# Weighting the expert outputs in the tile loop and adding them into the normalised rows in memory, in a state-space and mixture-of-experts kernel

## The chip, the cores and the metric

The kernel is one launch on one core of a Trainium2 chip. The number is the device time of one execution, in microseconds (us). The kernel before was run three times: 622.35, 623.21 and 623.45 us, median 623.21.

## The reference

Two blocks follow each other, on 8 sequences of 512 tokens with 256 features (4,096 tokens in all). The second is the one that the change touches.

```python
x = x + layernorm(s4d_block(layernorm(x)))                 # the first block gives x1
x = x + layernorm(moe_block(layernorm(x)))

def moe_block(x, ln_g, ln_b, rW, rb, W1, b1, W2, b2):      # 8 experts, 2 chosen per token
    z = layernorm(x) * ln_g + ln_b
    probs = softmax(z @ rW + rb)
    topv, topi = top_k(probs, 2)
    w = one_hot_weights(topv, topi) / max(sum, 1e-08)
    hid = gelu(z @ W1[e] + b1[e])                           # erf form
    outs = hid @ W2[e] + b2[e]
    return x + sum_e(outs[e] * w[e])
```

For each token the kernel needs n = layernorm(x1), the outputs y of its two experts, their weights w, and at the end x1 + layernorm(n + w0 y0 + w1 y1).

## The kernel before, in words

A block of 512 tokens (one sequence b) lies in SBUF as 128 partitions x 4 rows x 256 floats, 512 KB. Five instruction streams are written by hand: SP (`block.sync`, issues the plain DMAs), ACT (`scalar`), DVE (`vector`), POOL (`gpsimd`), PE (`tensor`). Each runs in its written order; semaphores order them against each other. There is no scheduler.

**The first block and the routing** (L306 to L995). For each b the first block ends in `xs[b]` (x1) and ACT writes `zn` (L516), the normalised rows n, in four buffers: b = 0, 2, 4 share one, b = 1, 3, 5 the next, b = 6 and 7 have their own (`buf`, L285). DVE picks two experts per row and works out where each row belongs in the expert's region, and POOL scatters the 4 rows of 128 tokens twice, once per choice, into `z_rows` in DRAM (L1116, 64 indirect DMAs). A row of `z_rows` has two more floats, the token's number and its second expert. SP stores x1 to `x1_dram` (`store_x1`, L344) and loads the experts' weights (`load_expert`, L269) as buffers come free.

**The tile loop** (`tiles`, L256; 71 tiles of 128 rows of one expert, six to a round of the hardware loop). For tile t SP loads 128 rows (`load_z`, L377). DVE finds out whether the row came from the first or the second choice (`flag`, L1005) and writes the row number where its result goes, token + 4096 x choice, to `dest` (L1008). PE transposes (L1316), ACT applies gain and bias (L584), DVE splits into a high and a low part (L1013, L1015), PE makes the first product (L1329), DVE adds the bias (L1023), ACT takes the gelu (L598), PE transposes (L1338), ACT and DVE split (L592, L1028), PE makes the second product (L1348). DVE copies `dest` to `dst` (L1037) and writes the product plus bias to `y_sb` (L1038). POOL sends the 128 rows of `y_sb` to `y_rows` in DRAM with an indirect DMA (`scatter_y`, L1146), 1 KB per row. There are two buffers of each tile, and the stages of several tiles overlap: in round i PE transposes the input of tile i + 2 and makes the second product of tile i - 1. `scatter_y(t)` waits for `y_ready` and for the landing of the scatter of t - 1:

```python
pool.wait_ge(sem("y_ready"), t + 1)
if not early(t):
    pool.wait_ge(sem(f"y_out{1 - q}"), (t + q) * 8)
```

**The tail.** When all scatters have landed, SP loads both results of each token (`ya`, L410, 16 loads of 512 KB, throttled two pairs at a time) and x1 of b = 0 to 3 (L408, 2 MB). POOL makes diagonal matrices of the weights (`weights`, L1161, products with the identity), PE sums the two results times their weights (`mix`, L1356, 128 matmuls), ACT makes n again from x1 (`base`, L603), DVE adds the two (L1048) and takes mean and variance (L1052, L1057), ACT takes the root (L614), DVE makes scale and shift (`scale`, L1060), ACT applies them (L618), DVE adds x1 (`add`, L1071), SP stores (L414).

## Time and profile before

| | |
|---|---|
| median of 3 runs | 623.21 us |
| the profiled execution | 619.89 us |
| its span, first to last instruction | 618.3 us |
| PE busy | 481.2 us (78%) |
| DVE busy | 462.4 us (75%) |
| ACT busy | 347.4 us (56%) |
| POOL busy | 227.2 us (37%) |
| mean granted TensorE clock | 0.903 |

The profile is one execution. Its span leaves 1.6 us of its own time outside, and its own time is 3.3 us below the median. Busy time counts what an engine executes, not its waits. "Idle before" in a row is the time that the engine stood still ahead of that instruction, with what ended it. An average over the span says little here, because the three stages (first block and routing, tile loop, tail) have different limits; each is read in its own window.

### The profile page before, as it was taken

The numbers are of one execution on the slowest core, as the hardware profiler recorded it, in microseconds if no ns is written. First come the engines' busy times: TensorE is split into PE (matmuls) and PEld (weight loads), VectorE is DVE, ScalarE is ACT, GpSimd is POOL, SyncE is SP. The second block draws the span as 40 slices with busy tenths as digits, with TensorE's granted clock in tenths as the row PEclk, the third lists the DMA queues.
The fourth block names the chain that finished last, engine by engine and source line by source line (L and its number), as shares of the span: only waits on it lengthen the run. The fifth ranks groups of instructions, "written<-read, shape, count | busy, mean of one in ns | idle before, by whom it ended". The sixth has DMA issues, their size and how long they took to land. (4 is left out here: it accounts for less than half of the span.)

```text
span 618.3 us, 12465 instructions
## 1 busy us (share of the span) xinstructions
PE 481.2 (78%) x2841; PEld 416.0 (67%) x2842; DVE 462.4 (75%) x1412; ACT 347.4 (56%) x751; POOL 227.2 (37%) x195
## 2 busy tenths in 40 slices
PE   0379899769979673132899999999999999956850
PEld 0139888659868573131788898889888888845640
DVE  6999877997986953863577777778778777832885
ACT  6983755654765566522455555555555555561584
POOL 0000676236775854653023232232232232342410
PEclk9998999989989885555799999999999999996995
DMA  6206600201110878336222222222222222119923
GB/s 186 88 0 255 222 1 1 68 2 69 44 61 36 287 261 296 95 126 223 85 69 77 77 72 81 68 72 81 68 69 84 68 74 79 60 43 368 344 103 136
DMA packets 36827, 69.56 MB, mean 113 GB/s; under 512 B 7520, under 2 KB 23648, under 8 KB 36160
## 3 DMA queue, kind: packets, MB, share of 16 engines
q1 hardware_dynamic: 30320, 51.48, 25.1%
q0 software_dynamic: 6480, 17.77, 8.1%
q8 instruction: 11, 0.18, 0.1%
q14 instruction: 16, 0.13, 0.1%
HBM read 42.02 MB, written 27.21 MB: 112 GB/s over the span
## 5 line engine op out<-in xcount | busy, mean ns | idle before, releaser
L1152 POOL DMA_INDIRECT y_rows<-y_sb,dst x71 | 76.5, 1077 | 194.0 <-DVE y_sb L1038 140.1
L1329 PE MATMUL psum<-ws,z_hl 128*128 x426 | 119.9, 417 | 0.8 <-DVE z_hl L1015 0.8
L1348 PE MATMUL psum<-ws,h_hl 128*128 x852 | 115.9, 285 | 0.1
L1348 PEld LDWEIGHTS psum<-ws,h_hl 128*128 128x128 f32 x852 | 103.5, 189 | 0.3 <-issue 0.3
L1116 POOL DMA_INDIRECT z_rows<-zn,pos x64 | 75.5, 1180 | 41.3 <-DVE pos L878 24.8
L1329 PEld LDWEIGHTS psum<-ws,z_hl 128*128 128x128 f32 x426 | 76.9, 193 | 16.0 <-issue 1.5
L592 ACT CAST h_hl<-psum 128x512 fp32r<-128x512 f32 x71 | 41.7, 587 | 76.0 <-PE psum L1338 76.0
L1023 DVE TENSOR_TENSOR hb<-psum,b1r 128x512 f32<-128x512 f32 x71 | 49.1, 692 | 37.3 <-issue 34.0
L584 ACT ACTIVATE z_f<-psum,gb 128x128 f32<-128x128 f32 x142 | 57.1, 452 | 15.7 <-PE psum L1316 13.8
L598 ACT ACTIVATE hg<-hb 128x512 f32<-128x512 f32 x71 | 44.9, 632 | 33.3 <-DVE hb L1023 33.3
L1219 PE MATMUL psum<-pm,ft 128*128 128x256 f32 x256 | 60.2, 395 | 0.4 <-DVE tmp L837 0.3
L1248 PE MATMUL psum<-yf,it 128*128 128x256 f32 x256 | 59.3, 387 | 0.0
L1219 PEld LDWEIGHTS psum<-pm,ft 128*128 128x128 f32 x256 | 50.2, 198 | 8.3 <-issue 1.2
L1248 PEld LDWEIGHTS psum<-yf,it 128*128 128x128 f32 x256 | 48.6, 194 | 6.5 <-POOL yf L1103 0.2
L1028 DVE TENSOR_TENSOR h_hl<-psum,h_hl 128x512 fp32r<-128x512 f32 x71 | 48.3, 680 | 1.3 <-ACT h_hl L592 1.3
L1364 PE MATMUL psum<-ya,diag 128*128 (+1 forms) x128 | 31.9, 410 | 18.1 <-DMA ya<-y_rows 13.7
L1316 PE MATMUL psum<-ident,z_in 128*128 128x128 f32 x142 | 28.8, 286 | 21.5 <-DMA z_in<-z_rows 20.0
L1338 PE MATMUL psum<-ident,hg 128*128 128x128 f32 x284 | 43.0, 274 | 0.0
L1338 PEld LDWEIGHTS psum<-ident,hg 128*128 128x128 f32 x284 | 35.7, 141 | 9.9 <-issue 0.2
L1364 PEld LDWEIGHTS psum<-ya,diag 128*128 128x128 f32 x128 | 26.0, 207 | 23.7 <-issue 19.9
L1101 POOL TENSOR_TENSOR yf<-yf,tmp 128x512 f32<-128x512 f32 x16 | 20.4, 1274 | 40.8 <-DVE rs L930 24.3
L1109 POOL TENSOR_TENSOR pm<-xn 128x512 f32<-128x512 f32 x8 | 10.3, 1285 | 66.2 <-ACT xn L441 66.2
(205 smaller groups left out, 847.1 us busy)
## 6 DMA issues: line engine op xcount, KB each, us to landing
z_in<-z_rows SPq DMA_DIRECT2D x71, 129.0 KB, 2.0
w_raw<-in_dram SPq DMA_DIRECT2D x16, 512.0 KB, 5.4
ya<-y_rows SPq DMA_DIRECT2D x16, 512.0 KB, 5.5
xs<-in_dram SPq DMA_DIRECT2D x8, 512.0 KB, 5.4
x_dram<-xs SPq DMA_DIRECT2D x8, 512.0 KB, 7.0
x1m<-x_dram SPq DMA_DIRECT2D x2, 2048.0 KB, 8.4
out_dram<-acc SPq DMA_DIRECT2D x8, 512.0 KB, 2.6
b1r<-in_dram SPq DMA_DIRECT2D x8, 256.0 KB, 4.5
```

Source lines behind the costliest of these rows:

```text
L584: last = nc.scalar.activation(z_f[:, k], ps_z[q][:, k], ACT.Identity, bias=gb[:, 1, k:k + 1], scale=gb[:, 0, k:k + 1])
L598: nc.scalar.activation(hg[q][:, :], hb[:, :], ACT.Gelu).then_inc(sem("hg_ready"), 1)
L1023: V.tensor_tensor(hb[:, :], ps_h[q], b1r[:, bass.ds(e, 1)].rearrange("p a f -> p (a f)"), ALU.add).then_inc(sem("hb_ready"), 1)
L1028: V.tensor_tensor(h_hl[q][:, 1], ps_t[q], h_hl[q][:, 0].bitcast(F32), ALU.subtract).then_inc(sem("h_split"), 1)
L1116: pool.indirect_dma_start(z_rows, bass.IndirectOffsetOnAxis(ap=pos[row.par][:, i // 4, i % 4:i % 4 + 1], axis=0), zn[buf(row.b)][:, i % 4] ...
L1152: pool.indirect_dma_start(y_rows, bass.IndirectOffsetOnAxis(ap=dst[q][:, 0:1], axis=0), y_sb[q][:, :], None).then_inc(sem(f"y_out{q}"), 16)
L1219: last = TE.matmul(fw[u][c][:, k], ft[:, c, t, kt * P:(kt + 1) * P], pm[row.b][:, c, t], start=t == 0, stop=t == 1)
L1248: last = TE.matmul(iv[c][:, j * H:(j + 1) * H], it[:, c, k, j * P:(j + 1) * P], yf[row.par][:, c, k], start=k == 0, stop=k == KT - 1)
L1329: last = TE.matmul(ps_h[q], z_hl[q][:, a, k], w_at(e1, c, k * F, F), start=n == 0, stop=n == 5)
L1338: last = TE.transpose(ps_t[q][:, k], hg[q][:, k * P:(k + 1) * P], ident[:, :])
L1348: last = TE.matmul(ps_y[q], h_hl[q][:, a, k], w_at(e2, c, 1024 + k * H, H), start=n == 0, stop=n == 11)
L1364: last = TE.matmul(ps_mix[par][:, k * H:(k + 1) * H], diag[par][:, c, k], ya[:, bass.ds(n, 1), c, k].rearrange("p a h -> p (a h)"), start= ...
```

## The change

`y_rows` now holds one row per token (4,096, and 128 that catch padding) instead of two. SP stores the normalised rows `zn` of each b there, right behind x1, and each of the buffers may be written again only when its store has landed (ACT). The weights are written to `w_rows` in DRAM, one float per token and choice. In the tile loop POOL gathers the 128 weights of a tile (`gather_w`), ACT multiplies the tile's result by them into a third pair of buffers `yw`, POOL copies the token numbers to `dst` (DVE did a copy of this kind before), and the scatter to `y_rows` adds to what stands there (`compute_op=ALU.add`). In the tail SP loads one row per token, and the diagonal matrices, the products on PE, ACT's `base` and DVE's addition of the two are gone; the last addition of x1 moves from DVE to POOL. Expert 4 is loaded behind expert 5.

```diff
-TRASH = 2 * B * T
+TRASH = B * T
...
+            def store_rows(lo, hi):
+
+                for b in range(lo, hi):
+                    sp.wait_ge(sem("x1_ready"), b + 1)
+                    sp.dma_start(x1_dram[:, b], xs[b][:, :, :]).then_inc(sem("x1_stored"), 16)
+                    sp.wait_ge(sem("zn_ready"), b + 1)
+                    sp.dma_start(y_tok[:, b], zn[buf(b)][:, :, 0:H]).then_inc(sem(f"zn_stored{buf(b)}"), 16)
+                sp.wait_ge(sem("x1_stored"), 16 * hi)
+
+
+            store_rows(0, 4)
+            load_expert(sp, 5)
...
             sp.wait_ge(sem("kf_mm"), 2)
             sp.wait_ge(sem("fwd_mm"), 16)
             load_expert(sp, 4)
-
-            def store_x1(lo, hi):
-                for b in range(lo, hi):
-                    sp.wait_ge(sem("x1_ready"), b + 1)
-                    sp.dma_start(x1_dram[:, b], xs[b][:, :, :]).then_inc(sem("x1_stored"), 16)
-                sp.wait_ge(sem("x1_stored"), 16 * hi)
-
-
-            store_x1(0, 4)
-            sp.wait_ge(sem("zn_ready"), 4)
-            load_expert(sp, 5)
-            store_x1(4, 6)
+            store_rows(5, 6)
             sp.wait_ge(sem("zn_ready"), 6)
             sp.wait_ge(sem("mult_done"), 2 * B)
             load_expert(sp, 6)
...
-            store_x1(6, 8)
-            sp.wait_ge(sem("zn_ready"), B)
-            sp.wait_ge(sem("x1_ready"), B)
+            store_rows(6, 8)
...
+            sp.dma_start(y_rows[TRASH:TRASH + P, :], zpad[:, 0:H]).then_inc(sem("trash_set"), 16)
...
+            sp.wait_ge(sem("wgt_ready"), 1)
+            sp.dma_start(w_rows.rearrange("(c p n) o -> p c (n o)", c=2, p=P),
+                         wgt[:, 0:2].rearrange("p c b k -> p c (b k)")).then_inc(sem("w_stored"), 16)
...
             for n in range(B):
-                if n >= 2:
-                    sp.wait_ge(sem(f"y0_in{n % 2}"), 16 * (n // 2))
-                    sp.wait_ge(sem(f"y1_in{n % 2}"), 16 * (n // 2))
-                if n == 3:
+                if n == 2:
+                    sp.wait_ge(sem("x1_in"), 16)
                     sp.dma_start(x1m[:, 0:4], x1_dram[:, 0:4]).then_inc(sem("x1_in"), 16)
-                for c in (1, 0):
-                    sp.dma_start(ya[:, n, c], y_tok[:, B - 1 - n, c].rearrange("p (k h) -> p k h", k=4)).then_inc(
-                        sem(f"y{c}_in{n % 2}"), 16)
+                sp.dma_start(yr[:, n], y_tok[:, B - 1 - n]).then_inc(sem(f"y_in{n}"), 16)
...
                     act.wait_ge(sem(f"scattered{row.par}"), 64 * (row.b - row.par))
+                    act.wait_ge(sem(f"zn_stored{row.par}"), 8 * (row.b - row.par))
...
+                t, q = i - 2, par
+                if live(t):
+                    act.wait_ge(sem("y_ready"), t + 1)
+                    gate(act)
+                    act.wait_ge(sem(f"w_in{q}"), (t - q) * 8 + 16)
+                    if not early(t):
+
+                        act.wait_ge(sem("dst_set"), t)
+                    nc.scalar.activation(yw[q][:, :], y_sb[q][:, :], ACT.Identity, scale=wt[q][:, 0:1]).then_inc(sem("yw_ready"), 1)
...
-
-
...
+            def close(n):
+                act.wait_ge(sem("m_var"), n + 1)
+                nc.scalar.activation(rm[:, n % 2, 0, :], mvm[n % 2][:, :, 1], ACT.Sqrt, bias=eps[:, 0:1]).then_inc(sem("m_sd"), 1)
+                act.wait_ge(sem("m_rs"), n + 1)
                 for k in range(4):
...
+                    last = nc.scalar.activation(acc[:, n, k], yr[:, n, k], ACT.Identity,
+                                                bias=rm[:, n % 2, 2, k:k + 1], scale=rm[:, n % 2, 1, k:k + 1])
                 last.then_inc(sem("m_fin"), 1)
...
+            for n in range(B):
+                close(n)
...
+                    V.tensor_copy(row_of[:, bass.ds(t, 1)], z_in[q][:, H:H + 1])
...
                     if not early(t, 2):
-                        dve.wait_ge(sem(f"y_out{q}"), (t - q) * 8)
-                    gate(dve)
-                    V.tensor_copy(dst[q][:, :], dest[:, bass.ds(t, 1)])
+                        dve.wait_ge(sem("yw_ready"), t - 1)
                     V.tensor_tensor(y_sb[q][:, :], ps_y[q], b2r[:, bass.ds(e, 1)].rearrange("p a f -> p (a f)"),
                                     ALU.add).then_inc(sem("y_ready"), 1)
 
...
+            def spread_of(n):
+                dve.wait_ge(sem(f"y_in{n}"), 16)
+                if n > 1:
+                    dve.wait_ge(sem("m_sd"), n - 1)
                 for k in range(4):
-                    last = V.bn_stats(st[:, par, k, :], acc[:, bass.ds(b, 1), k].rearrange("p a h -> p (a h)"))
-                last.then_inc(sem("m_stat"), 1)
-                dve.wait_ge(sem("m_stat"), b + 1)
-                gate(dve)
+                    last = V.bn_stats(st[:, n % 4, k, :], yr[:, n, k])
+                do(last)
                 for k in range(4):
-                    last = V.bn_aggr(mvm[par][:, k, :], st[:, par, k, :])
+                    last = V.bn_aggr(mvm[n % 2][:, k, :], st[:, n % 4, k, :])
                 last.then_inc(sem("m_var"), 1)
 
...
+            def scale(n):
+                par = n % 2
+                dve.wait_ge(sem("m_sd"), n + 1)
+                if n > 1:
+                    dve.wait_ge(sem("m_fin"), n - 1)
+                do(V.reciprocal(rm[:, par, 1, :], rm[:, par, 0, :]))
+                do(V.scalar_tensor_tensor(rm[:, par, 2, :], mvm[par][:, :, 0], -1.0, rm[:, par, 1, :], ALU.mult, ALU.mult))
+                V.tensor_tensor(rm[:, par, 2, :], rm[:, par, 2, :], xb[:, B - 1 - n], ALU.add).then_inc(sem("m_rs"), 1)
+
+            spread_of(0)
+            for n in range(B):
+                if n + 1 < B:
+                    spread_of(n + 1)
+                scale(n)
...
+            def gather_w(t, q):
+
+                pool.wait_ge(sem("dest_ready"), t + 1)
+                if not early(t, 2):
+                    pool.wait_ge(sem(f"w_in{q}"), (t - q) * 8)
+                gate(pool)
+                G.tensor_copy(widx[q][:, :], dest[:, bass.ds(t, 1)]).then_inc(sem("widx_set"), 1)
+                pool.wait_ge(sem("widx_set"), t + 1)
+                gate(pool)
+                pool.indirect_dma_start(wt[q][:, 0:1], None, w_rows,
+                                        bass.IndirectOffsetOnAxis(ap=widx[q][:, 0:1], axis=0)).then_inc(sem(f"w_in{q}"), 16)
+
             def scatter_y(t, q):
-                pool.wait_ge(sem("y_ready"), t + 1)
+
+                pool.wait_ge(sem("yw_ready"), t + 1)
                 if not early(t):
-
                     pool.wait_ge(sem(f"y_out{1 - q}"), (t + q) * 8)
                 gate(pool)
+                G.tensor_copy(dst[q][:, :], row_of[:, bass.ds(t, 1)]).then_inc(sem("dst_set"), 1)
+                pool.wait_ge(sem("dst_set"), t + 1)
+                gate(pool)
                 pool.indirect_dma_start(y_rows, bass.IndirectOffsetOnAxis(ap=dst[q][:, 0:1], axis=0),
-                                        y_sb[q][:, :], None).then_inc(sem(f"y_out{q}"), 16)
-
+                                        yw[q][:, :], None, compute_op=ALU.add).then_inc(sem(f"y_out{q}"), 16)
+
+            pool.wait_ge(sem("w_stored"), 16)
+            gather_w(0, 0)
+            gather_w(1, 1)
+            for b in range(B - 2):
+                pool.wait_ge(sem(f"zn_stored{b % 2}"), 16 * (b // 2 + 1))
+            for i in (2, 3):
+                pool.wait_ge(sem(f"zn_stored{i}"), 16)
+            pool.wait_ge(sem("trash_set"), 16)
             scatter_y(0, 0)
-            with pool.Fori(0, (TILES - 1) // 2) as j:
+            gather_w(2, 0)
+            with pool.Fori(0, (TILES - 3) // 2) as j:
                 scatter_y(j * 2 + 1, 1)
+                gather_w(j * 2 + 3, 1)
                 scatter_y(j * 2 + 2, 0)
...
+                gather_w(j * 2 + 4, 0)
+            scatter_y(TILES - 2, 1)
+            scatter_y(TILES - 1, 0)
+
+            def add(n):
+                pool.wait_ge(sem("m_fin"), n + 1)
+                if n % 4 == 0:
+                    pool.wait_ge(sem("x1_in"), 16 + 4 * n)
+                G.tensor_tensor(acc[:, n], acc[:, n], x1m[:, B - 1 - n], ALU.add).then_inc(sem("m_out"), 1)
+
+            for n in range(B):
+                add(n)
...
-            pe.wait_ge(sem("y_ready"), TILES)
-            mix(0, 0)
-            mix(1, 1)
-            with pe.Fori(1, B // 2) as j:
-                mix(j * 2, 0)
-                mix(j * 2 + 1, 1)
```

In the loop on POOL there was this, for two tiles (`dst` holds row numbers, `y_sb` the result):

```order
L1156 ISA
L1150 REGISTER_ALU [waits y_ready]
L1152 DMA y_rows<-y_sb_163,dst_145 8320x256 [waits y_out0]
L1147 REGISTER_ALU
L1152 DMA y_rows<-y_sb_162,dst_144 8320x256 [waits y_ready,y_out1]
L1156 REGISTER_ALU
L1156 COMPARE_AND_BRANCH
```

The same place in the changed kernel, for one of the two tiles (`yw` is the weighted result, `wt` the weights, `widx` their row numbers):

```order
L1122 ISA [waits yw_ready,y_out1]
L1122 COPY dst_144<-row_of 128x1
L1125 DMA y_rows<-yw_151,dst_144 4224x256 [waits dst_set]
L1106 REGISTER_ALU
L1108 REGISTER_ALU [waits dest_ready]
L1110 ISA [waits w_in0]
L1110 COPY widx_147<-dest 128x1
L1113 DMA wt_149<-w_rows,widx_147 128x1 [waits widx_set]
L1138 REGISTER_ALU
L1138 COMPARE_AND_BRANCH
```

Where POOL had one DMA per tile behind one set of waits, it has two copies and two DMAs, each DMA behind a wait for the copy ahead of it, and the first copy behind the landing of the scatter before.

In ACT's tile loop one tile of the changed kernel reads as follows:

```order
L586 ACTIVATE z_f<-psum,gb 128x128 [waits z_split,tz_mm]
L586 ACTIVATE z_f<-psum,gb 128x128
L594 CAST h_hl_177<-psum 128x512 [waits l2_mm,th_mm]
L600 ACTIVATE hg_174<-hb 128x512 [waits th_mm,hb_ready]
L609 ACTIVATE yw_152<-y_sb_170,wt_150 128x256 [waits y_ready,dst_set,w_in1]
```

The last row is new. It is the weighting of the tile whose number is three below that of the gelu ahead of it, and it waits for POOL's copy for the tile before it (`dst_set`), which in turn stands behind a landing.

On DVE the tail of one sequence had a 1,024-element addition ahead of the statistics and one behind; now it is this:

```order
L1031 BN_STATS st<-yr 128x6 [waits m_sd,y_in4]
L1031 BN_STATS st<-yr 128x6 x3
L1034 BN_AGGR mvm_183<-st 128x2 [waits dve_seq]
L1034 BN_AGGR mvm_183<-st 128x2 x3
L1042 RECIPROCAL rm<-rm 128x4 [waits m_fin,m_sd]
L1043 SCALAR_TENSOR_TENSOR rm<-mvm_184,rm 128x4 [waits dve_seq]
L1044 TENSOR_TENSOR rm<-rm,xb 128x4 [waits dve_seq]
```

The statistics of a sequence (here the fifth) stand ahead of the scale and shift of the one before it.

## Rows read from the trace of the kernel before

**Rows 1.** The page, part 2: busy tenths in 40 slices of 15.5 us.
```profile
PE   0379899769979673132899999999999999956850
...
PEclk9998999989989885555799999999999999996995
```
**Rows 2.** Stretches: PE, PEld, DVE, ACT, POOL busy, PEclk, DMA share, GB/s.
```profile
289.00:306.00 17.00, 13.94 (x59) 10.75 (x59) 8.63 (x27) 6.78 (x15) 0.05 (x1) 0.65 0.45 162
306.00:550.00 244.00, 241.60 (x1648) 215.50 (x1646) 189.05 (x542) 134.26 (x271) 74.52 (x69) 1.00 0.24 73
556.20:618.30 62.10, 31.87 (x128) 26.04 (x128) 38.24 (x104) 29.85 (x63) 13.58 (x8) 0.77 0.62 237
```
**Rows 3.** Timeline of the loop: start, duration, engine, line, idle before.
```profile
440.25 0.43 DVE L1038 TENSOR_TENSOR y_sb<-psum,b2r 128x256 f32<-128x256 f32 x1
...
441.49 1.12 POOL L1152 DMA_INDIRECT y_rows<-y_sb,dst  x1 [3.22 <-DVE y_sb L1038]
...
443.11 1.64 PE L1329 MATMUL psum<-ws,z_hl 128*128 x6
...
444.85 1.12 POOL L1152 DMA_INDIRECT y_rows<-y_sb,dst  x1 [2.23 <-DMA y_rows<-y_sb,dst]
...
446.55 1.65 PE L1329 MATMUL psum<-ws,z_hl 128*128 x6
```
**Rows 4.** `y_rows` in the trace: what POOL waited for (us, times), time to landing.
```profile
  DMA y_rows<-y_sb,dst: 48.3, 21
...
DMA to landing us min/median/max: 2.4/2.6/10.8
```
**Rows 5.** Timeline of POOL: a memset, one routing scatter, the first and last scatters.
```profile
0.22 0.10 POOL L1437 MEMSET const-float32-0.0<- 128x1 f32 x1 [0.22 <-issue]
...
149.51 0.96 POOL L1116 DMA_INDIRECT z_rows<-zn,pos  x1 [0.30 <-issue]
...
305.95 1.18 POOL L1152 DMA_INDIRECT y_rows<-y_sb,dst  x1 [21.81 <-DVE y_sb L1038]
...
553.67 0.96 POOL L1152 DMA_INDIRECT y_rows<-y_sb,dst  x1 [2.22 <-issue]
```
**Rows 6.** The page, part 6: DMA issues, KB each, us to landing.
```profile
z_in<-z_rows SPq DMA_DIRECT2D x71, 129.0 KB, 2.0
```
**Rows 7.** Groups in the window 306:550: busy, mean ns, idle before.
```profile
L598 ACT ACTIVATE hg<-hb 128x512 f32<-128x512 f32 x68 | 43.0, 632 | 29.6 <-DVE hb L1023 29.6
...
L1038 DVE TENSOR_TENSOR y_sb<-psum,b2r 128x256 f32<-128x256 f32 x70 | 29.7, 424 | 0.0
```
**Rows 8.** Timeline at the loop's start: ACT's gelu of the fourth tile.
```profile
307.42 0.63 ACT L598 ACTIVATE hg<-hb 128x512 f32<-128x512 f32 x1 [0.59 <-DVE hb L1023]
```
**Rows 9.** Timeline of the tail: one sequence's statistics, the last sequence's end.
```profile
569.30 1.41 DVE L1052 BATCH_NORM_STATS2 st<-acc 128x6 f32<-128x256 f32 x4
570.85 0.38 DVE L1057 BATCH_NORM_AGGREGATE mvm<-st 128x2 f32<-128x6 f32 x4
...
610.67 0.28 ACT L614 ACTIVATE rm<-mvm,eps 128x4 f32<-128x4 f32 x1
...
611.71 2.07 ACT L618 ACTIVATE acc<-acc,rm 128x256 f32<-128x256 f32 x4 [0.76 <-DVE rm L1068]
613.81 1.23 DVE L1074 TENSOR_TENSOR acc<-acc,x1m 128x1024 f32<-128x1024 f32 x1 [1.01 <-ACT acc L618]
```
**Rows 10.** The page: GB/s of the slices; POOL's additions and products (mean ns).
```profile
GB/s 186 88 0 255 222 1 1 68 2 69 44 61 36 287 261 296 95 126 223 85 69 77 77 72 81 68 72 81 68 69 84 68 74 79 60 43 368 344 103 136
...
L1101 POOL TENSOR_TENSOR yf<-yf,tmp 128x512 f32<-128x512 f32 x16 | 20.4, 1274 | 40.8 <-DVE rs L930 24.3
...
L1166 POOL TENSOR_TENSOR diag<-ident,wgt 128x1024 f32<-128x1024 f32 x8 | 15.1, 1897 | 20.4 <-PE psum L1364 20.4
```
**Rows 11.** SP's waits in total: what stood between its issues.
```profile
SPq L341 <- PE psum L1219: 83.3, 1, 83.3
...
SPq L388 <- DMA z_rows<-zn,pos: 4.6, 1, 4.6
```

127 lines of the change are left out of this document (16 added, 111 removed).

## The prediction, written before the changed kernel ran

> **What bounds the kernel now.** I read the slices of the page first, then the stretches, then the timeline inside one stretch.
>
> From 309 us on PE is busy nearly all the time and has its full clock (tenths of 9 and 1.00, 2.4 GHz) up to the tail [rows 1, 2]. In the loop proper (306 to 550 us) it is busy 241.6 of 244.0 us. PE's first product of one tile starts at 443.11 and that of the next at 446.55: 3.44 us. Over the whole loop the scatters start 70 times between 305.95 and 553.67 [rows 5], which is 3.54 us per tile. So PE is the bound of the loop. What matters more for this change is the runner-up. A scatter on POOL may start only when the one before has landed. Between 441.49 and 444.85 it was that landing that released POOL [rows 3], and it was so 21 times [rows 4]. Such an interval is 3.36 us: the scatter lands 2.6 us after its start [rows 4], and some 0.8 us pass until the next starts. The same 0.8 us stands between the end of `y_sb` (440.25 + 0.43 = 440.68) and the scatter at 441.49 [rows 3], so it is what POOL needs from a released wait to the start of an indirect DMA. The chain of scatters thus has 3.54 - 3.36 = 0.18 us of slack per tile. POOL looks idle two thirds of the loop, but its idle time is the flight of the scatters.
>
> The tail, from the last landing (553.67 + 2.4 = 556.1) to 618.3, takes 62.2 us [rows 2, 5]. There a chain passes PE, DVE and ACT for each sequence, behind 8 MB of loads.
>
> **What the change takes away: the tail.** Per sequence the diagonal matrices, 16 matmuls, ACT's base and two DVE additions go. The new tail, step by step. SP issues the rows of sequences 0 and 1 in its order, then 2 MB of x1, then those of 2. These are 3.67 MB at 344 to 368 GB/s [rows 10], 10.2 us, and some 2 us until a landing is seen (as z_in [rows 6]): 12.3. DVE's statistics of sequence 2 (1.41 + 0.38 with a wait between them, 1.9 [rows 9]) stand ahead of the scale of sequence 1: 14.2. Scale and shift take 0.75 (from 610.67 + 0.28 to 611.71), ACT applies in 2.1: sequence 1 is through at 17.3. From there on each sequence costs ACT root, wait for DVE, apply: 610.67 to 613.78, 3.1, say 3.15 [rows 9]; six of them end at 36.2. DVE's statistics (1.9) lie beside ACT's apply (2.1), so they cost nothing; were ACT faster, DVE would be next. The last addition is now on POOL. Its 512-element addition takes 1.27, its 1,024-element product with broadcast operands 1.90 [rows 10]: I take 2 x 1.27 = 2.5, low end 1.9, and POOL hides all but the last. The store after it and the end take 618.3 - 615.04 = 3.2 [rows 9]. Sum 36.2 + 0.1 + 2.5 + 3.2 = 42.0 us instead of 62.2: **20.2 us gained** (39 to 46 us are possible).
>
> **What it adds: the loop.** Per tile:
> - DVE copies the token number and no longer the row number: nil. Its result now waits for `yw` of two tiles earlier, which matters only if ACT is late.
> - ACT weights the result, 128 x 256. The same shape takes DVE 0.42 [rows 7], ACT's half of z_f 0.45; with it ACT has some 2.5 of 3.5 us busy. Its idle time before the gelu (29.6 us in 68 tiles [rows 7]) covers it. It is queued ahead of the next tile's z_f, so a late `dst_set` holds up everything.
> - POOL: the chain scatter to scatter gets a copy and its semaphore. A small operation on POOL takes 0.10 [rows 5]; with its start and its semaphore I take 0.3 (low 0.15; high 0.9, if a wait before the DMA costs another 0.8).
> - The add: the DMA engines must also read the row that they add to. No row shows such a DMA. Low end 0, since the trace has the plain write and nothing makes a read and write shorter than it; high end 2.0, a whole load of the same 128 rows, as z_in [rows 6]. I take 0.6, nearer to the plain scatter, since the 128 rows are independent and their reads overlap.
>
> Chain per tile: 3.36 + 0.3 + 0.6 = **4.26, taken as 4.25 us**, 0.7 above what PE needs. The second bound is POOL's own queue: scatter 1.1, copy 0.15, 0.8 until the gather starts, gather 1.1, copy 0.15, 0.8 until the next scatter: 4.1. With the shortest DMAs (0.96 [rows 5]) and 0.75 for a start it is 3.8. The gather lies in the scatter's flight as long as the flight is longer; so the two bounds are not summed.
>
> The Trainium skill (Collectives: The Full Stack, "The bandwidth ceiling: the fold count and why AG ≠ RS ≠ AR") says that the add in a DMA engine costs nothing itself and only doubles the reads; with the 436 GB/s of its DMA page (DMA: Bandwidth & Descriptors, "Anatomy of one DMA") that is 0.3 us for 128 KB, an estimate from the page, and by it the chain would be 3.96 and POOL's queue of 4.1 the bound: 643 instead of 655. No row here shows an adding DMA.
>
> Start: the gelu of the fourth tile ends at 308.05 [rows 8], ACT's first weighting at 308.5, and with copy and start the first scatter goes at 309.5 instead of 305.95. Then 70 x 4.25 = 297.5: the last starts at 607.0 and lands at 610.2, 54.1 later than before.
>
> **Before the loop.** Eight stores of 512 KB are added. SP waited 83.3 us in one piece for the last forward product [rows 11], and the first of them and of x1 now go into that gap. ACT's new wait for a stored buffer should be covered, since the same buffer is scattered first, which takes eight DMAs of 1.26. Expert 4 is behind expert 5, and expert 7's load behind 512 KB more (1.4 us). SP waited 4.6 us for the scatters ahead of the first z_in [rows 11], which covers the padding store. I put the whole at 1 us (0 to 5).
>
> **Sum.** 618.3 + 54.1 - 20.2 + 1 = 653.2, and with the 1.6 us outside the span 654.8: **655 us**, against 619.9 of the profiled execution. The runs' median was 3.3 us above that; the forecast stands for both within that.
>
> **Rivals.**
> 1. *The add is cheap and POOL's queue is the bound*, 4.1 us per tile: 309.5 + 287 + 2.9 = 599.4; with 42.0, 1 and 1.6 it is 644. For it: the DMA engines are used to a quarter in the loop [rows 2].
> 2. *The add is dear.* It costs a whole load more, 2.0: 5.66 per tile, last landing 710.3, in all 755. A longer descriptor program on POOL for it (1.6 instead of 1.1) would give 4.6 to 4.8 and 680 to 695. For it: each row must be read before it is written, and POOL must describe both.
> 3. *The loop stays PE's (faster than before).* If the add costs under 0.2 us and the gather's and copies' starts are hidden by POOL's sequencer, the interval is 3.65: last landing 309.5 + 255.5 + 2.6 = 567.6, in all 612. It decides at an interval of 3.8 us, where 309.5 + 266 + 2.8 + 44.6 = 623. For it: a DMA behind another starts 0.30 us after it [rows 5] instead of 0.8. Against it: both new DMAs wait for a copy that ends just before.
> 4. *PE's clock falls* in the new gaps: the first product took 1.65 at full clock [rows 3]; at 1.2 GHz a tile needs about twice its 3.44 at most, nearer 6.1, and all takes about 785. Against it: at tenths of 6 and 7 of busy time the clock stayed at 9 [rows 1].
> 5. *The change doesn't shorten the tail*: its loads (x1 ahead of rows 2 to 7) starve DVE, and it stays at 62: 675.
>
> **How the numbers follow.** Forecast (4.2 to 4.5 per tile) 0.38; rival 1 0.20; rival 2 0.22; rival 3 0.14; rival 4 0.02; rival 5 0.04. The likeliest case alone gives 636 to 690. The range leaves out most of rival 3 and the upper part of rival 2: 620 to 735. About 0.2% (1.2 us) is what a measurement of this kernel can tell from no change. Rival 3 is faster nearly wholly (0.13); between 622 and 624.5 lies almost nothing (0.03); slower 0.84.
>
> **What would show it.** Right: scatters over 4 us apart, POOL waiting for the landing of `y_rows`; PE's idle time in the loop ended by ACT or DVE, PE at 80 to 85% there and its clock full; ACT's `yw` released by POOL's `dst`; tail of about 42 us with POOL's addition at its end. If POOL is busy or starting something all the time and the landing is never last, rival 1 is right; if scatters land 4 us or more after their start, rival 2. Wrong: scatters 3.5 us apart, PE at 99%.

## The result, and the profile after

The changed kernel takes 729.70 us (median of 4 runs, 727.96 to 731.32), the kernel before, run beside it, 622.78 (620.24 to 623.45): a ratio of 1.171, interval 1.168 to 1.174. The sign was forecast and the range (620 to 735) holds it, but the forecast of 655 is 75 us too low. The profiled execution has a span of 729.3 us, 111.0 more than before.

The page of the changed kernel, busy tenths in slices of 18.2 us (compare [rows 1]):
```profile
PE   0678998798986330698877878778787877761000
...
POOL 0004572457576475145556566565656656664253
PEclk9989999898997555699999999999999999995555
```
In the loop PE is at 7 to 8 tenths and its clock stays at 9. The loop's stretch says it in numbers (PE, PEld, DVE, ACT, POOL busy, PEclk, DMA share, GB/s; compare [rows 2]):
```profile
306.00:640.00 334.00, 269.20 (x1613) 210.19 (x1611) 179.76 (x533) 153.70 (x332) 194.64 (x255) 0.99 0.32 51
```
PE fell from 99% to 81% of the loop at full clock, POOL rose from 31% to 58%. The costliest groups of the page (busy, mean ns, idle before and its releaser; compare [rows 7]):
```profile
L1125 POOL DMA_INDIRECT y_rows<-yw,dst x71 | 113.7, 1601 | 59.1 <-DVE dest L992 46.8
...
L1113 POOL DMA_INDIRECT wt<-w_rows,widx x71 | 71.3, 1004 | 59.2 <-POOL widx L1110 52.4
...
L609 ACT ACTIVATE yw<-y_sb,wt 128x256 f32<-128x256 f32 x71 | 36.1, 509 | 96.0 <-DMA wt<-w_rows,widx 96.0
...
L1110 POOL COPY widx<-dest 128x1 uint32 (+1 forms) x71 | 57.8, 814 | 13.3 <-DMA w_rows<-wgt 13.3
```
The adding scatter occupies POOL 1.60 us; it was 1.0 to 1.2 before. A copy of one number per partition takes 0.81. One tile on POOL, with the next scatter (start, duration, idle before; compare [rows 3]):
```profile
439.13 1.60 POOL L1125 DMA_INDIRECT y_rows<-yw,dst  x1 [0.82 <-DVE dest L992]
440.17 0.77 POOL L1110 COPY widx<-dest 128x1 uint32 x1
441.72 1.00 POOL L1113 DMA_INDIRECT wt<-w_rows,widx  x1 [0.79 <-POOL widx L1110]
443.30 0.18 POOL L1122 COPY dst<-row_of 128x1 uint32 x1 [0.58 <-DMA y_rows<-yw,dst]
444.31 1.59 POOL L1125 DMA_INDIRECT y_rows<-yw,dst  x1 [0.83 <-POOL dst L1122]
```
From 439.13 to 444.31 it is 5.18 us. The row of POOL's own work, scatter to copy 1.04, copy 0.77, start 0.79, gather 1.00, copy 0.18, start 0.83, is 4.6 of that. The 0.58 left is the wait for the landing of the scatter before. The copy `widx` lies partly inside the scatter's 1.60 and is slow there; the copy `dst`, alone, takes 0.18. Between 330 and 640 us POOL stood still before this copy in 56 tiles, 23.8 us in all, 0.4 each. The profile names the landing as what ended it in 10 of them and names nothing in 46, so this trace alone doesn't settle what binds; the run without gathers below does.

The beginning of the loop on POOL (compare [rows 5]):
```profile
302.82 0.18 POOL L1110 COPY widx<-dest 128x1 uint32<-128x1 uint32 x1 [13.25 <-DMA w_rows<-wgt]
...
315.93 1.77 POOL L1125 DMA_INDIRECT y_rows<-yw,dst  x1 [0.82 <-POOL dst L1122]
```
One sequence of the tail, DVE, ACT and POOL, up to the next addition (compare [rows 9]):
```profile
694.02 0.28 ACT L617 ACTIVATE rm<-mvm,eps 128x4 f32<-128x4 f32 x1
694.19 2.34 POOL L1150 TENSOR_TENSOR acc<-acc,x1m 128x1024 f32<-128x1024 f32 x1 [3.40 <-ACT acc L620]
694.33 0.18 DVE L1042 RECIPROCAL rm<-rm 128x4 f32<-128x4 f32 x1 [0.59 <-ACT rm L617]
694.54 2.00 DVE L1043 SCALAR_TENSOR_TENSOR rm<-mvm,rm 128x4 f32<-128x4 f32 x1
696.58 0.16 DVE L1044 TENSOR_TENSOR rm<-rm,xb 128x4 f32<-128x4 f32 x1
...
696.78 2.07 ACT L620 ACTIVATE acc<-yr,rm 128x256 f32<-128x256 f32 x4 [2.48 <-DVE rm L1044]
698.93 2.34 POOL L1150 TENSOR_TENSOR acc<-acc,x1m 128x1024 f32<-128x1024 f32 x1 [2.40 <-ACT acc L620]
```
DVE's product of 4 numbers per partition takes 2.00 us. The same line takes 0.16 where POOL does nothing beside it (691.64 in the same trace). It ends when POOL's addition ends (694.19 + 2.34 = 696.53), and ACT's apply stands behind it. So a sequence is 698.93 - 694.19 = 4.74 us.

Against the profiled execution of before the 111.0 us divide as follows: the first scatter is 10.0 later (315.93, 305.95 before), the 70 intervals take 358.8 instead of 247.7 (+111.1), from the last scatter to the tail's first load it is 4.0 instead of 2.4 (+1.5), and the tail takes 50.6 instead of 62.2 (-11.6).

### The profile page after: what moved, and what is told of

It reads as the page before. It is cut to its first block, busy times and chain, and to the rows that moved or that the text cites. A ratio compares the mean times of both kernels' runs of the same rounds, so it can differ in the third digit from the quotient of the medians.

```text
span 729.3 us, 12843 instructions
## 1 busy us (share of the span) xinstructions
PE 488.3 (67%) x2713; PEld 394.4 (54%) x2714; DVE 447.4 (61%) x1394; ACT 353.8 (49%) x788; POOL 370.7 (51%) x408
## 3 DMA queue, kind: packets, MB, share of 16 engines
q0 software_dynamic: 15568, 17.81, 14.9%
## 4 chain that ended last, share of the span: by engine, by line
DMA 26%; issue 22%; DVE 17%; ACT 11%; PE 11%; POOL 7%; POOLq 3%; SPq 1%; DVEq 1%; ACTq 0%
DMA y_rows<-yw,dst 22%; PE psum L1226 3%; POOL widx L1110 3%; PE psum L1197 3%; ACT acc L620 2%; POOL dst L1122 2%; DVE rm L1043 1%; PE psum L1184 1%; POOL z_rows L1074 1%; DMA yr<-y_rows 1%; ACT dump L549 1%; PE psum L1273 1%; DVE st L643 1%; DVE xs L905 1%; ACT dump L505 1%
## 5 line engine op out<-in xcount | busy, mean ns | idle before, releaser
L1307 PE MATMUL psum<-ws,z_hl 128*128 x426 | 121.5, 421 | 40.1 <-DVE z_hl L999 39.5
L1125 POOL DMA_INDIRECT y_rows<-yw,dst x71 | 113.7, 1601 | 59.1 <-DVE dest L992 46.8
L1113 POOL DMA_INDIRECT wt<-w_rows,widx x71 | 71.3, 1004 | 59.2 <-POOL widx L1110 52.4
L997 DVE CAST z_hl<-z_f 128x256 fp32r<-128x256 f32 x71 | 22.1, 311 | 114.7 <-ACT z_f L586 112.6
L609 ACT ACTIVATE yw<-y_sb,wt 128x256 f32<-128x256 f32 x71 | 36.1, 509 | 96.0 <-DMA wt<-w_rows,widx 96.0
L1110 POOL COPY widx<-dest 128x1 uint32 (+1 forms) x71 | 57.8, 814 | 13.3 <-DMA w_rows<-wgt 13.3
L1197 PE MATMUL psum<-pm,ft 128*128 128x256 f32 x256 | 62.2, 404 | 0.4 <-DVE tmp L823 0.4
L1316 PE MATMUL psum<-ident,hg 128*128 128x128 f32 x284 | 46.1, 285 | 8.0 <-ACT hg L600 2.5
L1316 PEld LDWEIGHTS psum<-ident,hg 128*128 128x128 f32 x284 | 31.2, 142 | 35.0 <-issue 18.6
```

The lines of the kernel that those rows point to most:

```text
L1110: G.tensor_copy(widx[q][:, :], dest[:, bass.ds(t, 1)]).then_inc(sem("widx_set"), 1)
L1113: pool.indirect_dma_start(wt[q][:, 0:1], None, w_rows, bass.IndirectOffsetOnAxis(ap=widx[q][:, 0:1], axis=0)).then_inc(sem(f"w_in{q}"), 16)
L1125: pool.indirect_dma_start(y_rows, bass.IndirectOffsetOnAxis(ap=dst[q][:, 0:1], axis=0), yw[q][:, :], None, compute_op=ALU.add).then_inc(se ...
L1197: last = TE.matmul(fw[u][c][:, k], ft[:, c, t, kt * P:(kt + 1) * P], pm[row.b][:, c, t], start=t == 0, stop=t == 1)
L1307: last = TE.matmul(ps_h[q], z_hl[q][:, a, k], w_at(e1, c, k * F, F), start=n == 0, stop=n == 5)
L1316: last = TE.transpose(ps_t[q][:, k], hg[q][:, k * P:(k + 1) * P], ident[:, :])
```

## The experiments

An interval is the time from the first to the last scatter over 70. "Landing" is the median from a scatter's start to its landing. The eight rows from "without the add" to "half rows, no gathers" are one run each, with 623.5 us for the kernel before beside them; the other times are medians of several. The columns behind the time are from the one execution that was profiled. Two cells are empty, since the view's median there, 10.1 us in the change and 5.1 without the add, isn't a flight: in the change POOL's copy behind the landing starts 4.17 us after the scatter (443.30 - 439.13), and no landing can be later than that.

| kernel | us | first and last scatter | interval | landing |
|---|---|---|---|---|
| before | 622.8 | 306.0, 553.7 | 3.54 | 2.6 |
| after | 729.7 | 315.9, 674.7 | 5.13 | |
| without the add | 654.9 | 312.8, 601.0 | 4.12 | |
| without gathers | 725.2 | 315.8, 668.4 | 5.04 | 3.8 |
| without both | 634.1 | 311.5, 575.3 | 3.77 | 2.5 |
| the same, copy on DVE | 652.8 | 311.5, 593.7 | 4.03 | 2.9 |
| two arrays | 697.3 | 312.8, 641.0 | 4.69 | 3.9 |
| two arrays, no gathers | 628.9 | 312.8, 572.4 | 3.71 | 4.6 |
| copy early, no gathers | 694.0 | 313.3, 637.2 | 4.63 | 3.8 |
| half rows, no gathers | 690.8 | 316.4, 634.3 | 4.54 | 3.3 |
| old loop in the new kernel | 603.4 | 307.7, 558.3 | 3.58 | 2.6 |

**Without the add.**
```diff
-                                        yw[q][:, :], None, compute_op=ALU.add).then_inc(sem(f"y_out{q}"), 16)
+                                        yw[q][:, :], None).then_inc(sem(f"y_out{q}"), 16)
```


> The changed kernel with the scatters writing plainly instead of adding (the rows keep only what was written last); everything else is as in the changed kernel. Theory A (the landing of the adding scatter sets the interval: 3.9 us of flight and 1.2 us until the next starts, 5.1): the flight falls back to some 2.6, the interval to 3.8 us, the whole to about 637 us. Theory B (POOL's own queue sets it: scatter 1.6, two copies, two starts of 0.8, gather 1.0): POOL's instruction falls from 1.6 to 1.1 us, the interval to 4.6, the whole to about 692 us.

Measured: 654.9 us, interval 4.12. POOL's timeline:
```profile
439.09 1.00 POOL L1125 DMA_INDIRECT y_rows<-yw,dst  x1 [0.82 <-POOL dst L1122]
440.09 0.20 POOL L1110 COPY widx<-dest 128x1 uint32 x1
441.07 1.03 POOL L1113 DMA_INDIRECT wt<-w_rows,widx  x1 [0.78 <-POOL widx L1110]
442.10 0.20 POOL L1122 COPY dst<-row_of 128x1 uint32 x1
443.12 1.00 POOL L1125 DMA_INDIRECT y_rows<-yw,dst  x1 [0.82 <-POOL dst L1122]
```
No landing stands in it: scatter, copy, start, gather, copy, start follow each other in 4.03 us. This is the 4.1 of the prediction's POOL row. Neither expectation was met. Theory A has the chain without the add right (3.8), but leaves out POOL's queue behind it; theory B has the right bound and makes it 4.6, because it lets only the scatter's instruction get shorter, while the copy `widx` falls from 0.77 to 0.20 as well. So the add itself costs 1.0 us per tile (5.13 - 4.12), 75 us in all.

**Without the gathers**, and **without both**. All weights are 0.5; the second also takes the add away as above.
```diff
-                pool.indirect_dma_start(wt[q][:, 0:1], None, w_rows,
-                                        bass.IndirectOffsetOnAxis(ap=widx[q][:, 0:1], axis=0)).then_inc(sem(f"w_in{q}"), 16)
...
-                    act.wait_ge(sem(f"w_in{q}"), (t - q) * 8 + 16)
```


> The changed kernel without the 71 gathers of weights and their copies of row numbers on POOL; every weight is the constant 0.5, so the outputs are not weighted as in the reference. Theory A: the interval stays at 5.0 to 5.1 us, the whole at 722 to 730 us. Theory B: POOL's queue shrinks to 2.8 us per tile, PE becomes the bound with 3.54 us, the whole falls to about 620 us.

> Both at once: plain scatters, no gathers, constant weights. Theory A: 2.6 of flight and 1.2 until the next start, interval 3.8 us, about 637 us. Theory B: PE's 3.54 us, about 620 us. If both bounds were equally near in the changed kernel, this one falls much further than either part alone.

Measured: 725.2 and 634.1 us, theory A in both (3.77 us for the interval of the second, 3.8 expected). Taking the gathers out of the changed kernel gains only 0.09 us per tile, though they are 1.8 us of POOL's row: the landing chain alone is 5.04. POOL's timeline without gathers, and the landings (us, min/median/max) without gathers:
```profile
439.82 0.18 POOL L1112 COPY dst<-row_of 128x1 uint32 x1 [2.41 <-DMA y_rows<-yw,dst]
440.80 1.56 POOL L1115 DMA_INDIRECT y_rows<-yw,dst  x1 [0.79 <-ACT yw L608]
...
DMA to landing us min/median/max: 2.9/3.8/14.0
```
Without both:
```profile
DMA to landing us min/median/max: 2.4/2.5/14.1
```
The add puts 1.3 us on a scatter's way from start to landing (3.8 against 2.5) and 0.5 on POOL's instruction (1.56 against 0.98 to 1.10). A landing is counted from the start of the instruction, so the 0.5 may lie inside the 1.3; no run separates the two. In the chain the add is worth 1.27 (5.04 - 3.77). And a chain without it is 3.77, where the prediction has 3.36 + 0.3 = 3.66.

**The old loop's order with ACT's weighting kept** (no add, no gathers, the copy of the token number back on DVE).
```diff
+                        dve.wait_ge(sem(f"y_out{q}"), (t - q) * 8)
+                    gate(dve)
+                    V.tensor_copy(dst[q][:, :], row_of[:, bass.ds(t, 1)])
```


> As noadd_nogather, and the copy of row numbers is back on DVE, ahead of the result, so that POOL's loop is again one DMA per tile; left of the change in the loop is ACT's weighting with a constant. If ACT's weighting is hidden, the interval is PE's 3.54 us and the whole about 615 us; if it is not, about 0.5 us per tile more, 650 us.

Measured: 652.8 us, interval 4.03. That is the second of the two expectations, 0.5 us per tile and 650 us for a weighting that isn't hidden. In the timeline DVE's copy for tile t waits for the landing of the scatter of t - 2, the result stands behind the copy, ACT's weighting 3.4 us behind the result, and the scatter behind that: a ring of two tiles in 8.1 us. It comes from this edit, since with the copy on POOL the interval was 3.77. The run of the old loop below has the same copy on DVE without the weighting.

**Two arrays, without and with the gathers.** Odd tiles add into a second array, which is initialised in the same way and which the tail leaves out, so that a scatter need wait only for the landing two tiles back. ACT's weighting waits for that landing too, where it waited for POOL's copy; the run with the copy early, below, has the same edit on ACT.
```diff
-                if not early(t):
-                    pool.wait_ge(sem(f"y_out{1 - q}"), (t + q) * 8)
+                if not early(t, 2):
+                    pool.wait_ge(sem(f"y_out{q}"), (t - q) * 8)
...
-                pool.indirect_dma_start(y_rows, bass.IndirectOffsetOnAxis(ap=dst[q][:, 0:1], axis=0),
+                pool.indirect_dma_start((y_rows, y_rows2)[q], bass.IndirectOffsetOnAxis(ap=dst[q][:, 0:1], axis=0),
```


> Leaves out the gathers of the weights (all weights are 0.5), and the tail leaves out a second array, y_rows2, also initialised with the normalised rows: the scatters of odd tiles add into it. So a scatter waits for the landing of the one two tiles earlier and no longer for the one before it; the adds are all there. A (each scatter waits for the landing of the one before; that chain, with the copy and the start behind it, is the 5.0 us per tile that the run without gathers still had): the wait is gone, POOL's own work is 1.56 + 0.2 + 0.8 us, and the interval is PE's, 3.55 to 3.7 us, in all 620 to 635 us. B (the adding scatters themselves are slow in the DMA engines, one after the other, whatever waits for them): the interval stays at 4.5 or more, in all 690 to 725. The second array costs eight more stores of 512 KB ahead of the loop, up to 5 us, in both.

> The same second array (which the tail leaves out), with the gathers of the weights. A (two bounds of nearly the same size, the landing chain and POOL's own row of two copies and two indirect DMAs): with the first gone the second stays, which adds up in the trace of the changed kernel to 1.04 + 0.77 + 0.79 + 1.00 + 0.18 + 0.82 = 4.6 us per tile; in all 690 to 705 us. C (POOL's work is hidden behind the flight, and only the landing counts): the interval falls to 3.6, in all 620 to 635.

Measured: 628.9 and 697.3 us, expectation A in both. With the wait for the last landing gone and all 71 adds still there, the interval falls from 5.04 to 3.71: the DMA engines are not what limits, the order of the adds is. Two of them are then in flight together, and a landing takes 4.6 instead of 3.8:
```profile
DMA to landing us min/median/max: 3.0/4.6/14.6
```
With the gathers back it is 4.69, POOL's row, as it was added up from the changed kernel's trace. POOL with two arrays and gathers:
```profile
439.72 1.59 POOL L1129 DMA_INDIRECT y_rows<-yw,dst  x1 [0.83 <-POOL dst L1126]
440.76 0.75 POOL L1114 COPY widx<-dest 128x1 uint32 x1
442.30 1.00 POOL L1117 DMA_INDIRECT wt<-w_rows,widx  x1 [0.79 <-POOL widx L1114]
443.30 0.20 POOL L1126 COPY dst<-row_of 128x1 uint32 x1
444.31 1.60 POOL L1129 DMA_INDIRECT y_rows<-yw,dst  x1 [0.82 <-POOL dst L1126]
```
So there are two bounds, 5.04 and 4.69, and each hides the other: taking one away alone gains 0.1 or 0.4 us per tile, both together 1.4.

**The copy ahead of the wait for the landing** (no gathers).
```diff
-                if not early(t):
-                    pool.wait_ge(sem(f"y_out{1 - q}"), (t + q) * 8)
                 gate(pool)
                 G.tensor_copy(dst[q][:, :], row_of[:, bass.ds(t, 1)]).then_inc(sem("dst_set"), 1)
                 pool.wait_ge(sem("dst_set"), t + 1)
+                if not early(t):
+                    pool.wait_ge(sem(f"y_out{1 - q}"), (t + q) * 8)
```


> Leaves out the gathers (all weights are 0.5) and puts POOL's copy of the token numbers ahead of the wait for the landing instead of behind it; ACT then waits for the landing two tiles back itself. A: the copy and its semaphore stand in the chain with 0.2 (landing to copy) + 0.18 us, so the interval falls from 5.04 by 0.2 to 0.4, to 4.65 to 4.85, in all 698 to 712. D (the 0.8 us of start runs from the last wait, the copy was not in series with anything): unchanged, 5.0 and 723 to 727.

Measured: 694.0 us, interval 4.63 instead of 5.04, slightly below what A expected (4.65 to 4.85, 698 to 712 us). The copy and its semaphores cost the chain 0.41 us; the prediction took 0.3. What is left is 3.8 for the landing and 0.8 for the start. ACT's edit is the same as with two arrays, so the step from 4.63 to 3.71 comes from the landing that is waited for, the last or the one before it.

**Half of each row added** (no gathers). The row number counts half rows here, so the adds also fall into the first half of the array.
```diff
-                pool.indirect_dma_start(y_rows, bass.IndirectOffsetOnAxis(ap=dst[q][:, 0:1], axis=0),
-                                        yw[q][:, :], None, compute_op=ALU.add).then_inc(sem(f"y_out{q}"), 16)
+                pool.indirect_dma_start(y_rows.rearrange("r (a c) -> (r a) c", a=2), bass.IndirectOffsetOnAxis(ap=dst[q][:, 0:1], axis=0),
+                                        yw[q][:, 0:P], None, compute_op=ALU.add).then_inc(sem(f"y_out{q}"), 16)
```


> Leaves out the gathers (all weights are 0.5) and half of what each scatter adds: 128 rows of 512 bytes instead of 1,024. A1 (the add's price is by row: so many small packets, each a read and a write): the flight stays at 3.8 us, the interval at 5.0, in all 720 to 727. A2 (it is by the byte): of the 0.8 us that the add put on the flight half goes, and the time of the payload too, so the flight is 3.2 to 3.4, the interval 4.5 to 4.65, in all 685 to 700. POOL's instruction stays at 1.56 in both, since it describes as many rows.

Measured: 690.8 us, landing 3.3 instead of 3.8, POOL's instruction 1.56 as before. The page's count of packets on that queue is 13,296 in both; so half the bytes in as many packets take 0.5 us less. So the landing depends on the bytes, as A2 has it (3.2 to 3.4, 690.8 us in its 685 to 700), though with half the bytes it is still 0.8 above the plain scatter of whole rows; POOL's part doesn't depend on them. How much of the 0.5 a plain scatter of half the bytes would also save was not tried.

**The tail: one source, and the addition back on DVE.**
```diff
-                do(V.scalar_tensor_tensor(rm[:, par, 2, :], mvm[par][:, :, 0], -1.0, rm[:, par, 1, :], ALU.mult, ALU.mult))
-                V.tensor_tensor(rm[:, par, 2, :], rm[:, par, 2, :], xb[:, B - 1 - n], ALU.add).then_inc(sem("m_rs"), 1)
+                for k in range(4):
+                    last = V.tensor_scalar(rm[:, par, 3, k:k + 1], rm[:, par, 1, k:k + 1], -1.0, None, ALU.mult)
+                do(last)
+                for k in range(4):
+                    last = V.tensor_scalar(rm[:, par, 2, k:k + 1], mvm[par][:, k, 0:1], rm[:, par, 3, k:k + 1],
+                                           xb[:, B - 1 - n, k:k + 1], ALU.mult, ALU.add)
+                last.then_inc(sem("m_rs"), 1)
```


> In the tail of the changed kernel DVE's two small operations with two SBUF inputs (the product that makes the shift, and its sum with the offset) become eight with one SBUF tensor and at most two scalars per partition. E (DVE's instruction with two SBUF inputs stands still while POOL's addition runs, 2.00 instead of 0.16 us, and so each sequence takes 4.74 us): the stall goes, eight small ones cost 0.8 instead of 0.3, the sequence takes 3.3 to 3.7 us, the tail from the last landing 50.7 becomes 43 to 45, and all 721 to 724 us instead of 729.7. F (the stall is of the place, not of the operands: any DVE operation there waits for POOL): one of the eight takes 2 us, and the time stays within 1 us of 729.7.

Measured: 723.1 us (722.1 to 723.6; ratio to before 1.164, 1.161 to 1.166). The timeline:
```profile
695.35 2.34 POOL L1155 TENSOR_TENSOR acc<-acc,x1m 128x1024 f32<-128x1024 f32 x1 [1.39 <-ACT acc L620]
695.49 0.18 DVE L1042 RECIPROCAL rm<-rm 128x4 f32<-128x4 f32 x1 [0.60 <-ACT rm L617]
695.70 0.34 DVE L1044 TENSOR_SCALAR rm<-rm 128x1 f32<-128x1 f32 x4
696.08 0.82 DVE L1047 TENSOR_SCALAR rm<-mvm,rm,xb 128x1 f32<-128x1 f32 x4
...
699.08 2.34 POOL L1155 TENSOR_TENSOR acc<-acc,x1m 128x1024 f32<-128x1024 f32 x1 [1.39 <-ACT acc L620]
```
All eight run beside POOL's addition and none is held; a sequence takes 3.73 instead of 4.74 us. So it isn't the place that waits for POOL, but the operation with two inputs from SBUF (E). The eight also differ from the two in shape, 128x1 for 128x4; that the inputs decide and not the shape is supported by DVE's reciprocal of 128x4, which has one input and isn't held at 695.49.

In the other run the last addition is on DVE again, all else as in the change.
```diff
+            def add(n):
+                dve.wait_ge(sem("m_fin"), n + 1)
...
+                V.tensor_tensor(acc[:, n], acc[:, n], x1m[:, B - 1 - n], ALU.add).then_inc(sem("m_out"), 1)
```


> The last addition of x1 goes back from POOL to DVE; all else is the changed kernel. E: without an operation on POOL nothing stalls DVE; a sequence is DVE's addition 1.23, statistics 1.85 and scale and shift 0.6 to 0.7, in all 3.7 to 3.9 us instead of 4.74, and the last addition takes 1.23 instead of 2.34: all 722 to 725 us. G (the move to POOL was worth what it took from DVE): 730 or more.

Measured: 715.8 us (714.8 to 718.9; 1.154, 1.150 to 1.157), 14 us less than the change and more than was expected. DVE's line, whole for one sequence:
```profile
689.77 0.16 DVE L1043 SCALAR_TENSOR_TENSOR rm<-mvm,rm 128x4 f32<-128x4 f32 x1
689.97 0.16 DVE L1044 TENSOR_TENSOR rm<-rm,xb 128x4 f32<-128x4 f32 x1
690.05 1.22 DVE L1050 TENSOR_TENSOR acc<-acc,x1m 128x1024 f32<-128x1024 f32 x1
691.18 1.40 DVE L1031 BATCH_NORM_STATS2 st<-yr 128x6 f32<-128x256 f32 x4
...
693.09 0.16 DVE L1043 SCALAR_TENSOR_TENSOR rm<-mvm,rm 128x4 f32<-128x4 f32 x1
```
A sequence is 3.32 us (693.09 - 689.77): DVE's operations follow without gaps, each starting at the end of the other or slightly before. The tail, from SP's first load (673.46) to the end (712.7), is 39.2 us. Of the 16.6 us between the two spans (729.3 - 712.7) 11.4 lie in the tail and 4.7 in an earlier first scatter (311.2), which this edit does not touch.

**The old loop in the new kernel.** Scatters of the unweighted result overwrite, as before, so that the tail normalises one expert's result per token; weighting, gathers, add and both copies on POOL are left out; the copy of the row number and the last addition are on DVE.
```diff
-                pool.wait_ge(sem("yw_ready"), t + 1)
+                pool.wait_ge(sem("y_ready"), t + 1)
...
-                                        yw[q][:, :], None, compute_op=ALU.add).then_inc(sem(f"y_out{q}"), 16)
+                                        y_sb[q][:, :], None).then_inc(sem(f"y_out{q}"), 16)
```


> Leaves out the weighting and the adding: scatters of the unweighted results overwrite, as the kernel before does, so that y_rows holds one expert's result per token, and the tail normalises that. The loop is the one of before (the row number copied by DVE, one DMA on POOL per tile), all the rest is the changed kernel with its last addition on DVE. H (the loop's 111 us all come from the three added steps, weighting, gather and add; the stores ahead of the loop cost 0 to 3 us; the tail is 39 us instead of 62): interval 3.54, 283.8 + 24 to 27 + 247.7 + 2.6 + 39.2 + 2 = 599 to 603 us, and with it the ring through ACT's weighting was what held the run with the plain loop at 4.03. I (DVE's copy behind the landing two tiles back, or the new stores, cost by themselves): interval 3.8 or more, 618 or more.

Measured: 603.4 us (602.5 to 604.4), before 623.8 beside it, ratio 0.967 (0.964 to 0.970), which is H within 0.4 us of its range; the interval is 3.58. The loop's stretch:
```profile
306.00:550.00 244.00, 240.12 (x1627) 213.35 (x1625) 189.58 (x608) 132.60 (x271) 76.24 (x68) 1.00 0.24 72
```
PE is back at 98%. DVE's copy behind the landing two tiles back costs nothing by itself; the 4.03 above needs the weighting beside it. So the shorter tail and the new stores together are worth 20 us of gain, and the three steps in the loop, with their copies, lose 112 (712.7 - 600.7, both with the same tail).

**The last addition on POOL in the kernel before.** Four kernels, all with the tail loops written out (`b_unroll` is that alone).
```diff
-                add(j * 2)
...
+            for n in range(2, B):
+                weights(n, n % 2)
+                add(n - 2)
```


> The kernel before with the tail loops of its engines written out, no instruction else changed. It is the control for the next one. The chain of the tail of before shows few gaps at the loops' ends, 1 us at most in all: 0 to 2 us faster than before, 621.5 to 623.5.

> The kernel before, tail written out, with its last addition of x1 on POOL instead of DVE, and the shift by the eight operations with one SBUF tensor. From 590 us on a sequence of before takes 5.2 us, DVE's row of two additions, statistics and shift. E: DVE loses 1.23 and gains 0.5 us, is never held by POOL, and ACT's row of apply, base and root (4.4 us) becomes the bound: 0.7 us less in each of five sequences, 1.1 more for the last addition: 619 to 621 us, faster than both kernels. F (POOL holds DVE all the same, or POOL's 1.9 + 2.34 us per sequence become the bound): 622 to 627.

Measured: 620.9 (ratio to before 0.998, 0.995 to 1.000, so no difference is shown) and 648.1 us (1.043, 1.041 to 1.045). The second missed both expectations. POOL's timeline shows additions and matrices in turn, with 7 us of waiting every second sequence: the matrices of sequence n stood behind the addition of n - 3, and PE's products behind the matrices.
```diff
+            weights(2, 0)
+            weights(3, 1)
+            for n in range(B):
+                add(n)
+                if n + 4 < B:
+                    weights(n + 4, n % 2)
```


> The kernel before, tail written out, its last addition of x1 on POOL, and POOL's order mended: in the last run the diagonal matrices of sequence n stood behind the addition of sequence n - 3, and with the products of PE between them this was a ring of two sequences in 11.4 us. Now four sets of matrices stand ahead of the first addition, and those of n behind that of n - 4. J: the ring is gone, DVE's row is 0.7 us shorter per sequence, ACT's 4.4 us or POOL's 1.90 + 2.34 bind: 618 to 621 us against 620.9 of the tail written out alone. K (the last addition, 2.34 instead of 1.23, and DVE held by POOL in its remaining operations eat that): 621 to 626.

Measured: 629.5 us (1.008, 1.005 to 1.011): the mended order gives back 19 of the 27 us, but the time is above both J and K. A sequence now took 5.70 us: ACT's apply, base, root, and then its wait for DVE's scale. The last pair moves the root:
```diff
+                root(n, n % 2)
...
+                if n + 2 < B:
+                    base(n + 2)
+                apply(n, n % 2)
```


> The kernel before, tail written out, with one thing moved on ACT: the root of a sequence stands ahead of the base of the sequence two later instead of behind it, so that DVE's scale and shift run beside that base. L (ACT's row in the tail, apply 2.0, base 2.0, root 0.3 and then idle 0.75 for DVE, is what sets 5.2 us per sequence): the 0.75 is gone, DVE's row of two additions, statistics and scale, 4.9 to 5.0 us, is next; 0.2 to 0.3 us in each of some five sequences, 619 to 620.5 us, 1 to 2 less than before. M (DVE's row is the bound already): no change beyond 1 us.

> The same move on ACT, and the last addition of x1 on POOL in the mended order, with the shift by operations of one SBUF tensor. L: ACT 4.3, DVE 1.2 + 1.95 + 1.5 = 4.65, POOL 1.90 + 2.34 = 4.24 us per sequence: some 4.7 instead of 5.7 in the last run, 629.5 becomes 618 to 622, near or slightly below before. N (POOL's additions delay the matrices and so PE's products whatever ACT does): over 625.

Measured: 621.0 us (0.997, 0.995 to 0.999) with the root moved alone, and 629.1 (1.011, 1.008 to 1.014) with POOL's addition. The first is 0.3% faster than before, but it takes as long as the tail merely written out (620.9): beside that control the move gained nothing that can be told, which is M. L had 619 to 620.5. The second stays slow for the reason of N; PE's line there:
```profile
593.62 3.72 PE L1359 MATMUL psum<-ya,diag 128*128 128x256 f32 x16 [0.77 <-POOL diag L1152]
599.84 5.41 PE L1359 MATMUL psum<-ya,diag 128*128 128x256 f32 x16 [2.50 <-POOL diag L1152]
```
PE waits for POOL's matrices, which stand behind an addition of 2.36 us.

## Why the prediction was right in its direction and wrong in its size

The forecast span was 653.2 us and it is 729.3: 76.1 more. The largest term is the interval, 0.876 us too short: 0.67 of it is the add, 0.11 the copy and 0.09 POOL's queue, which are taken up one by one below. By the prediction's own terms:

| term | forecast | measured | miss |
|---|---|---|---|
| first scatter | 309.5 + 1 | 315.9 | 5.4 |
| 70 intervals | 4.25 each | 5.126 each | 61.3 |
| last scatter to the first load | 3.2 | 4.0 | 0.8 |
| tail | 42.0 | 50.6 | 8.6 |

**What bounds, and the mechanism: right.** The chain scatter, landing, copy, start, scatter became the bound of the loop; PE went to 81% with a full clock (0.99), as forecast (80 to 85%). Without the gathers the chain alone still gives 5.04. One of the signs named for it didn't come: ACT's `yw` was to be released by POOL's copy `dst`, and it was released by the landing of the gather (96.0 us of idle time, 68 times). The weighting at 444.07 waited for the gather of 441.72, while the copy of 443.30 had ended before. The prediction had no such wait. It stands beside the chain and not in it, since without the gathers the interval falls by 0.09 only.

**The add: the step that failed.** "I take 0.6, nearer to the plain scatter, since the 128 rows are independent and their reads overlap." It is 1.3 (3.8 against 2.5, and 5.04 against 3.77 in the interval), in the middle of the range of 0 to 2.0 that the rows allowed. The 0.7 between them is 49 us of the 61. Part of it can be the longer instruction on POOL (1.56 instead of 1.0 to 1.1), which the prediction left at 1.1. How much of the rest goes by the bytes stays open: with half of them the landing is 3.3. The reason given for the low value was an argument without a row. The Trainium skill's rule (Collectives: The Full Stack, "The bandwidth ceiling: the fold count and why AG ≠ RS ≠ AR"), by which the add only doubles the reads, was further off: 0.3 by the prediction's estimate from it.

**The copy in the chain** was to be 0.3 and is 0.41 (copy early). Together with the chain of before this makes 3.77 instead of 3.66.

**POOL's queue: right without the add, wrong with it.** 4.1 was forecast and 4.12 measured without the add. The prediction kept 1.1 for the adding scatter and put the longer instruction only into rival 2, "1.6 instead of 1.1 would give 4.6 to 4.8". It is 1.6 and the queue is 4.69. This bound lies under the chain's 5.04, and the two give 5.13 together.

**The statement that the two bounds are not summed: right**, nearly. 5.04 and 4.69 give 5.13, 0.09 above the larger.

**The start.** From the last routing scatter (288.6) to the first of the loop it is 27.3 us, before 22.8: 4.5 more, where 3.5 was forecast; in the other kernels with the old loop's first scatter it is 23.3 to 23.8, so about 1 of the 4.5 is this execution of before. The other 5.4 us of the 10.0 lie ahead of the last routing scatter (283.2 before). In the ten runs with the new stores of one array this scatter starts between 283.8 and 288.6, and in the kernels with the old code between 283.2 and 286.9. By the fastest of each, an estimate, the new stores cost 0.6 us, where 1 was forecast; the rest varies from execution to execution.

**The tail: right in its build, wrong in one term.** The second sequence was through 15.4 us after SP's first load (694.1 - 678.7), 17.3 forecast, and ACT's apply and root have their forecast lengths. What failed is "POOL hides all but the last": POOL's addition held DVE's two-input product for 1.84 us in each sequence, 4.74 instead of 3.15, six times 1.6. The last store and the end took 4.3 us where 3.2 was forecast. With the addition on DVE the tail is 39.2, less than the 42.0 forecast for POOL. The trace of before showed such a case that was not read: DVE L1068 takes 1.75 us at 575.09, beside POOL's matrices, and 0.16 elsewhere.
```profile
574.92 1.90 POOL L1166 TENSOR_TENSOR diag<-ident,wgt 128x1024 f32<-128x1024 f32 x1 [1.53 <-PE psum L1364]
575.09 1.75 DVE L1068 TENSOR_TENSOR rm<-rm,xb 128x4 f32<-128x4 f32 x1
```

**The rivals.** Rival 1 is what the run without the add does (654.9), not the change. Rival 2 is what happened, in its milder half: it put 680 to 695 on POOL's longer instruction and 755 on an add of 2.0. It had 0.22 where it deserved more, since it gave both prices and both came true in part. Rival 3 falls with the add, rival 4 with the clock at 0.99 (its argument read [rows 1] too well: of the five slices ahead of the tail in which PE is at 6 or 7 tenths four show a clock of 8 and one shows 9), rival 5 with the tail at 50.6.
